# Softmax attention: one more column of the values' low parts on GpSimd, the output's low rows added by accumulating transfers, the values' high parts copied by ScalarE

## The reference

```
h = layernorm(x)
q, k, v = (low-rank projections of h).reshape(b, s, 16, 64).transpose(0, 2, 1, 3)
q, k = rope(q), rope(k)
scores = einsum('bhqd,bhkd->bhqk', q, k) / sqrt(64)
attn = softmax(scores, axis=-1)
out = einsum('bhqk,bhkd->bhqd', attn, v)
out = out.reshape(b, s, 1024) @ w_out.T + x
```

## Time and profile before

| what | value |
|---|---|
| median of 3 runs | 4127.34 us (4121.48 to 4130.55) |
| time of the profiled execution | 4116.43 us |
| its span | 4114.6 us |
| instructions | 55305 |
| attention stage, first to last exponential | about 911 to 3629 us |

### The profile page before, as it was taken

How to read it: one execution, slowest core, us unless ns; L and a number is a source line. 1 busy time by engine, 2 the same in 40 slices (tenths; PEclk the granted TensorE clock), 3 DMA queues, 4 the chain that set the end, 5 groups by cost and what they waited for, 6 DMA issues and landing times. The chain is left out here.

```text
span 4114.6 us, 55305 instructions
## 1 busy us (share of the span) xinstructions
PE 3728.8 (91%) x17018; PEld 2904.5 (71%) x17018; DVE 3332.2 (81%) x4389; ACT 2623.4 (64%) x3395; POOL 3045.0 (74%) x2832
## 2 busy tenths in 40 slices
PE   7959996769999999999999999999999999989563
PEld 4634544548888888888888888888888888867321
DVE  7845557869999999999999999999999999946511
ACT  6723333327777777777777777777777777732221
POOL 2447775758888888888888888888888888820165
PEclk9969998979999999999999999999999999999776
DMA  8123437862322433234332333323332243156295
GB/s 276 48 63 62 65 59 245 266 205 60 67 60 58 94 64 66 59 68 85 65 65 60 77 78 66 65 60 81 74 64 63 60 88 68 44 173 205 79 241 108
DMA packets 332633, 396.27 MB, mean 96 GB/s; under 512 B 142540, under 2 KB 251921, under 8 KB 319283
## 3 DMA queue, kind: packets, MB, share of 16 engines
q1 hardware_dynamic: 307702, 362.22, 35.0%
q0 software_dynamic: 24640, 30.52, 4.3%
HBM read 232.47 MB, written 117.79 MB: 85 GB/s over the span
## 5 line engine op out<-in xcount | busy, mean ns | idle before, releaser
L1823 ACT ACTIVATE at_ph<-at_ps_s 128x1024 fp32r<-128x1024 f32 x1024 | 1053.0, 1028 | 572.6 <-PE at_ps_s L1875 550.8
L1732 DVE TENSOR_REDUCE at_mx<-at_ps_u 128x2 f32<-128x1024 f32 x1016 | 1241.0, 1221 | 152.4 <-PE at_ps_u L1858 122.9
L1752 DVE TENSOR_TENSOR at_pl<-at_ps_s,at_ph 128x1024 fp32r<-128x1024 f32 x1024 | 1248.9, 1220 | 20.4 <-ACT at_ps_s L1826 17.5
L1826 ACT ACTIVATE at_ps_s<-at_ps_s 128x1024 f32<-128x1024 f32 x1024 | 1032.2, 1008 | 32.5
L1661 POOL TENSOR_TENSOR at_part<-at_ph,at_vl 128x512 f32<-128x512 f32 x768 | 799.3, 1041 | 110.6 <-ACT at_ph L1823 81.5
L1669 POOL TENSOR_TENSOR at_acc<-at_acc,at_part 128x512 f32<-128x512 f32 x640 | 836.0, 1306 | 50.1
L1891 PE MATMUL at_ps_v<-at_pl,at_va 128*128 128x512 f32 x2048 | 810.1, 396 | 0.0
L1890 PE MATMUL at_ps_v<-at_ph,at_va 128*128 128x512 f32 x2048 | 808.2, 395 | 1.0 <-DVE at_pl L1752 1.0
L1893 PE MATMUL at_ps_v<-at_ph,at_vx 128*128 128x512 f32 x1152 | 453.4, 394 | 0.0
L1891 PEld LDWEIGHTS at_ps_v<-at_pl,at_va 128*128 128x128 f32 x2048 | 387.2, 189 | 88.3
L1890 PEld LDWEIGHTS at_ps_v<-at_ph,at_va 128*128 128x128 f32 x2048 | 387.6, 189 | 46.0 <-DVE at_pl L1752 1.7
(11 more groups left out here) (290 smaller groups left out, 5384.3 us busy)
## 6 DMA issues: line engine op xcount, KB each, us to landing
wgu<-Wgu_in SPq DMA_DIRECT2D x64, 384.0 KB, 5.5
qT<-pj_rot SPq DMA_DIRECT2D x32, 512.0 KB, 5.5
vT<-pj_vo SPq DMA_DIRECT2D x16, 1024.0 KB, 5.7
kT<-pj_rot SPq DMA_DIRECT2D x32, 512.0 KB, 3.2
k<-kT SPq DMA_DIRECT2D x32, 512.0 KB, 11.6
q<-qT SPq DMA_DIRECT2D x32, 512.0 KB, 9.6
at_q<-wup SPq DMA_DIRECT2D x128, 128.0 KB, 2.3
at_vf<-vT SPq DMA_DIRECT2D x32, 512.0 KB, 8.6
```

The lines of the kernel that those rows point to most:

```text
L1732: dve.tensor_reduce(mx[:, qb % 2, 2 * i:2 * i + 2], maxima_at(base, j)[:, 0:2], X, ALU.max).then_inc(s["u_max"], 1)
L1752: dve.tensor_tensor(pl[:, n % NP], ps_s[:, n % 2], ph[:, n % NP].bitcast(F32), ALU.subtract)\
L1823: act.activation(ph[:, n % NP], ps_s[:, n % 2], ACT.Exp, scale=DH ** -0.5)\
L1826: act.activation(ps_s[:, n % 2], ps_s[:, n % 2], ACT.Exp, scale=DH ** -0.5)\
```

## The change

- GpSimd takes chunk 14's low column too: SUMS is 8, `vx` has eight pieces and one matmul of a block (the second `vx` matmul of slot 7) goes. `own_products` is one copy where it was two.
- The fold of a block moves from slot 0 to slot 3 of the next one, and `output` from slot 2 to slot 5.
- `low_rows`, `whole`, `o_lo` and `o_st` go. `store_o` writes output rows 0 to 63 straight from `o_all` as soon as `output` is done. In slot 7 of a block GpSimd issues `add_low_rows` for the block before: a transfer of 63 rows by 512 from `o_all` to `o_dram` that adds to what is there; it waits until `store_o` has landed. `output` waits for the accumulating transfer of two blocks before.
- `split_values` moves from GpSimd's slots 16, 18, 20, 22 to ScalarE's slots 15, 17, 19, 21.

```diff
-        SUMS = PER - 1
+        SUMS = PER
         NX = 2 * PER - SUMS
-        TAIL = 3
+        TAIL = 4
...
-            o_lo = sb("o_lo", [DH, 2, QB])
-            o_st = sb("o_st", [DH, 2, QB])
...
             def own_product(c):
 
-                if c == KC - 2:
-                    return NX - 1
                 return c // 2 if c % 2 == 1 else None
...
-                def low_rows(block_):
-
-                    sp.wait_ge(s["o_ready"], block_ + 3)
-                    if block_ > 1:
-                        sp.wait_ge(s["o_added"], block_ - 1)
-                    sp.dma_start(o_lo[1:DH, block_ % 2], o_all[DH + 1:P, block_ % 2]).then_inc(s[f"o{block_ % 2}_low"], 16)
-
                 def store_o(pr, hh, qb):
-                    sp.wait_ge(s["o_added"], pr * (2 * NQB) + (hh * NQB + qb + 1))
+                    sp.wait_ge(s["o_ready"], pr * (2 * NQB) + (hh * NQB + qb + 3))
                     stand_alone(sp, s["turns"])
                     sp.dma_start(self.o_dram[bass.ds(pr, 1), hh * DH:(hh + 1) * DH, qb * QB:(qb + 1) * QB].squeeze(0),
-                                 o_st[0:DH, qb % 2]).then_inc(s[f"o{qb % 2}_out"], 16)
+                                 o_all[0:DH, qb % 2]).then_inc(s[f"o{qb % 2}_out"], 16)
...
-                        if block_ > 0:
-                            low_rows(block_ - 1)
...
+                for ob in range(2):
+                    sp.wait_ge(s[f"o{ob}_whole"], 32 * H)
...
-                    pool.tensor_copy(vx[:, hh, 0:NX - 1, 0:1], vl0[:, hh, 1::2].unsqueeze(2)).then_inc(s["vx_ready"], 1)
-                    pool.tensor_copy(vx[:, hh, NX - 1:, 0:1], vl0[:, hh, KC - 2:KC - 1].unsqueeze(2)).then_inc(s["vx_ready"], 1)
+                    pool.tensor_copy(vx[:, hh, :, 0:1], vl0[:, hh, 1::2].unsqueeze(2)).then_inc(s["vx_ready"], 1)
...
-                        if c < KC - 4:
+                        if c < KC - 2:
                             to = acc[:]
...
-                def whole(g, qb):
-
-                    pool.wait_ge(s[f"o{qb % 2}_low"], 16 * ((g * NQB + qb) // 2 + 1))
-                    pool.tensor_tensor(o_st[:, qb % 2], o_lo[:, qb % 2], o_all[0:DH, qb % 2], ALU.add).then_inc(s["o_added"], 1)
+                def add_low_rows(g, qb):
+
+                    pool.wait_ge(s[f"o{qb % 2}_out"], g * 64 + (32 * (qb // 2) + 64))
+                    pool.dma_start(self.o_dram[g // 2, g % 2 * DH + 1:(g % 2 + 1) * DH, qb * QB:(qb + 1) * QB],
+                                   o_all[DH + 1:P, qb % 2], accum_op=ALU.add).then_inc(s[f"o{qb % 2}_whole"], 16)
...
-                        if n % PER == 5 and g * NQB + n // PER > 0:
-                            whole((g * NQB + n // PER - 1) // NQB, (n // PER - 1) % NQB)
+                        if n % PER == 7 and g * NQB + n // PER > 0:
+                            add_low_rows((g * NQB + n // PER - 1) // NQB, (n // PER - 1) % NQB)
...
                         if 0 <= i < 2 * NQB:
-                            if i % 2 == 0:
-                                split_values(nxt, 1 - hh, pr + hh, i // 2)
-                            else:
+                            if i % 2 == 1:
                                 low_values(nxt, 1 - hh, i // 2)
...
                 def output(g, qb):
                     act.wait_ge(s["fold_done"], g * NQB + qb + 1)
                     act.wait_ge(s[f"o{qb % 2}_out"], g * 64 + (32 * (qb // 2) + 32))
+                    if g * NQB + qb > 1:
+                        act.wait_ge(s[f"o{qb % 2}_whole"], g * 32 + 16 * (qb // 2))
                     act.activation(o_all[:, qb % 2], ps_v[:, qb % 2], ACT.Copy).then_inc(s["o_ready"], 1)
+
+                def split_values(g, hh, half, i):
+                    if i == 0:
+                        act.wait_ge(s[f"v{hh}"], half * 16 + 16)
+                        if g > 0:
+                            act.wait_ge(s["pv_done"], g * SLOTS + (NP - SLOTS))
+                    at = slice(i * VQ, (i + 1) * VQ)
+                    act.activation(va[:, hh, at, 0:DH], vf[:, hh, at], ACT.Copy).then_inc(s["vh_ready"], 1)
...
-                        if n % PER == 2 and n > PER:
+                        i = n % SLOTS - SLOTS // 2 + 1
+                        if 0 <= i < 2 * NQB and i % 2 == 0 and 2 * pr + n // SLOTS + 1 < HEADS:
+                            split_values(2 * pr + n // SLOTS + 1, 1 - n // SLOTS, pr + n // SLOTS, i // 2)
+                        if n % PER == 5 and n > PER:
                             output(pr * 2 + (n - PER) // SLOTS, (n - PER) % SLOTS // PER)
...
-                        if n % PER == 0 and g * NQB + n // PER > 0:
+                        if n % PER == 3 and g * NQB + n // PER > 0:
                             fold(g * NQB + n // PER - 1)
```

More of the change, by code:

```diff
@@ L1461, in softmax_attention @@
             names = ("turns raw0 raw1 kq0 kq1 v0 v1 fixed cut_ready low_ready low0 low1 u_full u_max mg_ready nm_ready "
-                     "row0 row1 row2 row3 s_full p_ready pf_ready pl_ready vh_ready v_split pv_done scaled sums vl0_ready vx_ready fold_done o_added o0_low o1_low "
-                     "next_in pick_in pick_out o_ready o0_out o1_out den recip rden").split()
+                     "row0 row1 row2 row3 s_full p_ready pf_ready pl_ready vh_ready v_split pv_done scaled sums vl0_ready vx_ready fold_done "
+                     "next_in pick_in pick_out o_ready o0_out o1_out o0_whole o1_whole den recip rden").split()
             s = {n: sem(n) for n in names}
@@ L1475, in sums_before @@
                 return n // PER * SUMS + sum(own_product(c) is None for c in range(2 * (n % PER)))
+            VQ = KC // NQB
             def loaded(eng, name, hh, half, each):
@@ L1589, in _ @@
                 head(PAIRS - 1, 1, False, True)
-                low_rows(HEADS * NQB - 1)
                 store_o(PAIRS - 1, 1, NQB - 1)
@@ L1593, in _ @@
                     sp.wait_ge(s[f"o{ob}_out"], 32 + 32 * HEADS * NQB // 2)
+                    sp.wait_ge(s[f"o{ob}_whole"], 16 * HEADS * NQB // 2)
                 sp.wait_ge(s["next_in"], 48)
@@ L1602, in _ @@
                 link(pool.memset(first[:, 0:1].bitcast(F32), 1.0))
-                link(pool.memset(o_lo[:], 0.0))
                 for i in range(2):
                     link(pool.memset(k2[i][MROW:MROW + 2, :].bitcast(F32), 1.0))
-                VQ = KC // NQB
-                def split_values(g, hh, half, i):
-                    if i == 0:
-                        pool.wait_ge(s[f"v{hh}"], half * 16 + 16)
-                        if g > 0:
-                            pool.wait_ge(s["pv_done"], g * SLOTS + (NP - SLOTS))
-                    at = slice(i * VQ, (i + 1) * VQ)
-                    pool.tensor_copy(va[:, hh, at, 0:DH], vf[:, hh, at]).then_inc(s["vh_ready"], 1)
                 def low_values(g, hh, i):
@@ L1698, in _ @@
                 for i in range(NQB):
-                    split_values(0, 0, 0, i)
                     low_values(0, 0, i)
@@ L1707, in _ @@
                 head(PAIRS - 1, 1, False)
-                whole(HEADS - 1, NQB - 1)
+                add_low_rows(HEADS - 1, NQB - 1)
             @block.vector
@@ L1788, in reciprocals @@
                         dve.tensor_tensor(rl[:], rd[:], rh[:].bitcast(F32), ALU.subtract).then_inc(s["recip"], 1)
-                dve.wait_ge(s["fixed"], 7)
+                dve.wait_ge(s["fixed"], 6)
                 for i in range(NQB):
@@ L1827, in pair @@
                             .then_inc(s["pf_ready"], 1)
-                        if n % PER == 2 and n > PER:
+                        i = n % SLOTS - SLOTS // 2 + 1
+                        if 0 <= i < 2 * NQB and i % 2 == 0 and 2 * pr + n // SLOTS + 1 < HEADS:
+                            split_values(2 * pr + n // SLOTS + 1, 1 - n // SLOTS, pr + n // SLOTS, i // 2)
+                        if n % PER == 5 and n > PER:
                             output(pr * 2 + (n - PER) // SLOTS, (n - PER) % SLOTS // PER)
-                        elif n == 2 and pr > 0:
+                        elif n == 5 and pr > 0:
                             output(pr * 2 - 1, NQB - 1)
+                for i in range(NQB):
+                    split_values(0, 0, 0, i)
                 for pr in range(PAIRS):
@@ L1840, in _ @@
             def _(pe):
-                pe.wait_ge(s["fixed"], 7)
+                pe.wait_ge(s["fixed"], 6)
                 def products(base, hh, half, j):
@@ L1883, in values @@
                             pe.wait_ge(s["v_split"], g * NQB + NQB)
-                            pe.wait_ge(s["vx_ready"], 2 * (g + 1))
+                            pe.wait_ge(s["vx_ready"], g + 1)
                         if c2 == 0:
```

## The result

The changed kernel's median is 4143.34 us (4137.04 to 4147.97), against 4121.48 us (4116.44 to 4130.55) for the kernel before on the same chip: ratio 1.0044, 95% interval 1.0032 to 1.0055. It is slower, by some 20 us (21.9 between the medians, 18 by the ratio) where +38 was forecast. 4143 lies inside the range of 4100 to 4225 and inside the forecast's own range of 4132 to 4207.

What follows compares the result with a forecast made beforehand. TensorE bounds the kernel by little; the change makes GpSimd the bound at 86.3 us a head against 85.0. +40 for 31 heads and -2 for the last give +38 on 4127.34: 4165 us, 8-in-10 range 4100 to 4225.

Steps and rivals of the forecast that it cites:

- the forecast's own range: Whole kernel with GpSimd as the bound and a transfer of 0.6 to 1.2 us: +5 to +80 us; chance 0.55.
- GpSimd becomes the bound: Attention stage: GpSimd needs 86.3 us a head against 85.0 now, +1.3 us in each of 31 heads, +40 us.
- The accumulating transfer, 1.08 each: On GpSimd, four a head: 0.87 us plus gaps of 0.16 and 0.02 and lost overlap 0.04; 4.3 us a head.
- my terms: GpSimd's start-to-start prices: full slot 2.56 us, first slot 1.18, interrupted 2.37 and 0.98, `take_low` 1.26, transfer 1.08.
- Rival 1: Faster: transfer descriptors cost GpSimd's chain next to nothing; 4097 us, or 4113 at 0.43 each in proportion to rows; chance 0.20.
- rival 3: Much slower: transfers at 1.73 us plus gap 0.30 give 4290 us, or late store landings at most +150; chance 0.11.
- Rival 2: No change: transfers at about 0.55 us, or the gain eaten by held-up cuts; 4127 us within 8; chance 0.14.
- The last head and the end, -2: Last head prepares nothing, so GpSimd takes 80.0 us, 5 less; 3 given back for the late last fold.
- TensorE "alone would need 84.0", stalls of 1.3 stay: TensorE in a head: one matmul less a block saves 0.93 us; the 1.3 us of stalls, mostly from cuts, remain.
- VectorE's cuts, up to 1.53 each: Four cuts a head, held up by GpSimd: at most 4.4 us more on VectorE, 84.4, still below 86.3.
- Zeros: Parts priced at nothing: ScalarE's four copies of 0.40 us, `add_low_rows` waiting for the store, `output` waiting for an earlier transfer.
- What the column was expected to bring: TensorE: one `vx` matmul less per block, 0.93 us a head, 30 us over 32 heads while TensorE is the bound.

Runs made afterwards that it cites:

- the run without transfers: The changed kernel with the accumulating transfers left out, so output rows 1 to 63 lack their low parts: 4063.79 us, ratio 0.9859, head 83.60 us.
- three blocks of four: The changed kernel with the eighth column on GpSimd in three of a head's four blocks and seven in the other: 4087.99 us, ratio 0.9915.
- seven columns: The changed kernel with seven columns on GpSimd in every block, chunk 14 back on TensorE's old matmul: 4101.57 us, ratio 0.9957.

## Why the prediction was right and wrong

- **GpSimd becomes the bound: right.** Its idle time fell from 206.7 us to 2.5 in the window, ScalarE waits for it 154 times instead of 21, and the column moved back in one block makes TensorE the bound again. TensorE's share in the window fell to 98.2%; I said 97.
- **The accumulating transfer, 1.08 each: the step that failed.** The term was right in kind and too large: measured 0.80 for each one added, 0.78 in the mean by the local times below. The transfer itself takes 0.83 (0.87 was taken), but it isn't alone on the engine: the product behind starts 0.56 after it. I had read the gaps ahead of and behind the plain scatters as costs on top, and in those rows no product of this width follows. By the same pieces, local times are 3.28 where my terms give 3.51, twice a head, as much less at a third place (3.95 for 4.18), and 4.06 where they give 4.57, once: -1.2 us a head, of a forecast of +1.3. On the other side there are hold-ups around the cuts, which I had priced at zero for GpSimd. GpSimd after, in time order, from the product above on:

```profile
2138.88 1.30 POOL L1640 TENSOR_TENSOR at_part<-at_ph,at_vl 128x512 f32<-128x512 f32 x1
2140.25 1.34 POOL L1648 TENSOR_TENSOR at_acc<-at_acc,at_part 128x512 f32<-128x512 f32 x1
2141.73 1.04 POOL L1640 TENSOR_TENSOR at_part<-at_ph,at_vl 128x512 f32<-128x512 f32 x1
...
2146.47 1.34 POOL L1648 TENSOR_TENSOR at_acc<-at_acc,at_part 128x512 f32<-128x512 f32 x1
2147.95 1.04 POOL L1640 TENSOR_TENSOR at_part<-at_ph,at_vl 128x512 f32<-128x512 f32 x1
...
2151.58 1.22 POOL L1640 TENSOR_TENSOR at_part<-at_ph,at_vl 128x512 f32<-128x512 f32 x1
2152.88 1.30 POOL L1648 TENSOR_TENSOR at_acc<-at_acc,at_part 128x512 f32<-128x512 f32 x1
```

Product to sum is 1.37 and 1.30 here where 1.12 is usual, sum to product twice 1.48 where 1.44 is: 0.5 in this head. 86.3 - 1.2 + 0.5 = 85.6, measured 85.57. So +0.49 a head over 85.08, not +1.3. The whole forecast was the small difference between 86.3 and 85.0: an error of 0.3 in a term that comes four times is nearly all of it. Without the hold-ups of 0.5, which I had not counted either, the kernel would have been no slower a head than before (85.1 against 85.08), so that half of the forecast came true is partly luck.
- **By rows or by transfer.** Rival 1 weighed 0.43 for 63 rows, in proportion. 31, 32 and 63 rows each hold the list 0.55 to 0.56 us to the next start, and four transfers more cost 0.80 each with the same rows in all: no proportion. Rival 1 does not hold, nor does rival 3's dearest row of 1.73. Rival 2's transfer of about 0.55 with its gaps, 0.77, is near the measured price; its "no change" did not come because of the hold-ups and the stage's end.
- **The last head and the end, -2: wrong.** The last head won 1.3, but the end lost 8.2. I counted the fold that comes late (3 us given back) and not the transfer of the last block, which now stands behind the store and on GpSimd, nor the drain. GpSimd's last sum, which had ended 1.9 us behind the last exponential, ended 7.4 behind it. Some 7 us of the 20.7.
- **TensorE "alone would need 84.0", stalls of 1.3 stay: wrong in size.** The runs in which TensorE is the bound have stalls of 0.8 to 1.0. With 356 matmuls it would need 83.6, not 84.0 (the run without transfers). More was to be won than rival 1 said (0.9859, 58 us), but only with a GpSimd that is no bound and with the transfers left out.
- **VectorE's cuts, up to 1.53 each: right in direction, and not quite hidden.** Their mean is 1.27, up from 0.73 (41.4 us in 56 and 39.4 in 54), and the longest 2.49, up from 1.53. VectorE has 52 us more in the window, 1.8 a head, for which the cuts account: (1.27 - 0.73) x 4 = 2.1. Added up it stays below GpSimd's list, as said, but TensorE waits longer for VectorE's maxima: its weight loads 79.2 us in the window where it was 28.3. With the column in three blocks of four, and GpSimd busy 2237 of 2400 us, a cut takes 0.69. The Trainium skill (SBUF — State Buffer, Who interferes with whom) says that when VectorE is in a two-port mode, whichever of the two engines issues first has the shared ports for its whole instruction and the other waits. By that rule the trace agrees for 1.27, which is less than the 0.42 alone plus one sum of 1.30; the longest of 2.49 is more than that, so one GpSimd instruction ahead doesn't account for it.
- **Zeros.** ScalarE's four copies: right (409 ns each, and no row of the waits names them). The store's landing: right; `add_low_rows` waits 0.3 us in the whole window. The transfer's own landing takes 3.1 us in the median (3.0 to 10.4) and nobody waits for it except at the stage's end. The Trainium skill (DMA: Bandwidth & Descriptors, Anatomy of one DMA — SWDGE (gpsimd) path) gives a transfer that GpSimd issues 2.0 us plus its bytes over 436,000 to the microsecond, as an estimate 2.3 us for these 129 KB; the measured 3.1 is longer.
- **What the column was expected to bring** (0.93 us a head, 30 us in all) is there for the most part where TensorE is the bound: against seven columns the run without transfers gains 0.84 a head, three blocks of four 0.54 of 0.70. In the change as made it is lost because GpSimd's list, 85.6, is 2 us longer than TensorE's 83.6.

## What to carry to other kernels

Where two engines are within 2 or 3% of each other (85.6 and 83.6 us here), price the chain from start to start, and price an instruction that no row shows as a gap between its neighbours, with the next instruction beside it, not as its duration plus gaps. Move work between such engines in steps small enough to stop at the balance: three blocks of four gave 0.9915 where four gave 1.0044. And when an instruction is moved to a later slot, read the queue behind everything that waits for it: one store that waited two slots longer cost 7.5 us a head through the loads behind it.

## What the runs showed of the hardware, unexpected

- An accumulating transfer more in GpSimd's list costs it 0.80 us where the list is the bound (88.79 - 85.57 for four) and nothing where it isn't (84.45 against 84.44). From its start to the next instruction's it is 0.55 to 0.56 us for 31, 32 and 63 rows of 2 KB alike; its record of 0.83 us overlaps the next instruction by 0.27, which takes 1.35 where it takes 1.04 elsewhere.
- After such transfers GpSimd's drain at a stage's end takes 7.2 to 9.4 us instead of 1.35 to 1.39, and it ends 8.4 us behind the issue of a transfer that closes the list (two kernels), 6.0 us behind the end of an addition that closes it (one kernel).
- With GpSimd never idle, a cut on VectorE takes 1.27 us in the mean, three times its shortest of 0.41; it took 0.73 before, with GpSimd busy 2106 of 2400 us.
